# Group 0 in two halves, W on ScalarE's DMA queue, sums three tiles behind, gathers spread over the group two ahead, and a rearranged tail, in a DLRM tower on one core

## The reference

```python
def _cin_layer(X0, Xi, W, b):            # X0 (512,39,16), Xi (512,Fi,16), W (128, 39*Fi)
    Wr = W.reshape(H, F0_, Fi)
    return jnp.einsum('hjk,bjd,bkd->bhd', Wr, X0, Xi) + b[None, :, None]
e = jnp.stack([tbl_0[ids[:, 0]], ..., tbl_38[ids[:, 38]]], axis=1)
# three layers, each summed over d and concatenated: z (512, 384)
h = jnp.concatenate([z, dense_ctx], axis=1)          # (512, 400)
h = jnp.maximum(h @ W_top1 + b_top1, 0.0)            # 512 wide
h = jnp.maximum(h @ W_top2 + b_top2, 0.0)            # 256 wide
y = h @ W_top3
```

## Time and profile before

| | us |
|---|---|
| median of three timed runs | 673.68 (673.07 to 673.69) |
| the profiled execution | 672.67 |
| its span in the profile | 670.6 |
| busy: TensorE / VectorE / ScalarE / GpSimd | 641.9 / 521.2 / 488.3 / 361.1 |
| the first product of group 0's second layer | at 44.37 |
| the last chunk of the last group | at 611.8 |

### The profile page before, as it was taken

How to read it: one execution, slowest core, us unless ns; L and a number is a source line. 1 busy time by engine, 2 the same in 40 slices (tenths; PEclk the granted TensorE clock), 3 DMA queues, 4 the chain that set the end, 5 groups by cost and what they waited for, 6 DMA issues and landing times.

```text
span 670.6 us, 11899 instructions
## 1 busy us (share of the span) xinstructions
PE 641.9 (96%) x2516; PEld 461.4 (69%) x2516; DVE 521.2 (78%) x1478; ACT 488.3 (73%) x1692; POOL 361.1 (54%) x308
## 2 busy tenths in 40 slices
PE   0689999999999999999999999999999999999998
PEld 0246777777777777777777777777777777785483
DVE  0346888878888888888888878888888888897590
ACT  1137877778787868787877878787868787897293
POOL 6878766575656565755666675656575221121000
PEclk9799999999999999999999999999999999999999
DMA  6457687767676777667667767676777657567100
GB/s 225 60 92 168 112 183 133 173 131 162 124 160 128 159 150 163 142 134 155 139 144 134 167 130 161 124 160 129 160 150 162 142 102 178 126 122 215 31 1 0
DMA packets 61944, 91.05 MB, mean 136 GB/s; under 512 B 34599, under 2 KB 38548, under 8 KB 61671
## 3 DMA queue, kind: packets, MB, share of 16 engines
q0 software_dynamic: 14192, 51.02, 42.0%
q1 hardware_dynamic: 47734, 39.85, 21.2%
HBM read 10.59 MB, written 1.28 MB: 18 GB/s over the span
## 4 chain that ended last, share of the span: by engine, by line
PE 91%; POOL 3%; DMA 3%; issue 2%; SPq 1%; ACT 0%; DVE 0%; ACTq 0%; POOLq 0%
PE t_bank L426 22%; PE t_bank L427 21%; PE t_bank L428 21%; PE x_bank L394 14%; PE small_bank L411 5%; POOL emb L324 3%; PE t_bank L491 1%; PE t_bank L471 1%; PE t_bank L502 1%; PE t_bank L503 1%; PE t_bank L514 1%; PE t_bank L505 1%; DMA emb<-in_table,idx 1%; PE x0t_bank L402 1%; DMA emb_scratch<-emb 1%
## 5 line engine op out<-in xcount | busy, mean ns | idle before, releaser
L567 ACT ACTIVATE prod<-t_bank,x0t 128x128 f32<-128x128 f32 x1472 | 417.5, 377 | 114.6 <-PE t_bank L428 109.3
L671 DVE SCALAR_TENSOR_TENSOR prod<-t_bank,x0t,prod 128x128 f32<-128x128 f32 x1024 | 287.9, 343 | 80.1 <-PE t_bank L428 75.8
L426 PE MATMUL t_bank<-w_hi,x_hi 128*128 128x512 f32 (+1 forms) x640 | 307.5, 480 | 0.6 <-DVE x_lo L660 0.3
L427 PE MATMUL t_bank<-w_lo,x_hi 128*128 128x512 f32 (+1 forms) x640 | 247.8, 387 | 0.0
L428 PE MATMUL t_bank<-w_hi,x_lo 128*128 128x512 f32 (+1 forms) x640 | 247.0, 386 | 0.0
L324 POOL DMA_INDIRECT emb<-in_table,idx x160 | 211.8, 1324 | 48.5 <-issue 46.8
L334 POOL TENSOR_TENSOR diag<-x0t,mask 128x320 f32<-128x320 f32 x64 | 87.8, 1372 | 195.4 <-DVE prod L671 97.7
L426 PEld LDWEIGHTS t_bank<-w_hi,x_hi 128*128 128x128 f32 x640 | 120.2, 188 | 54.7 <-issue 29.7
L427 PEld LDWEIGHTS t_bank<-w_lo,x_hi 128*128 128x128 f32 x640 | 120.5, 188 | 47.1 <-issue 25.3
L428 PEld LDWEIGHTS t_bank<-w_hi,x_lo 128*128 128x128 f32 x640 | 120.1, 188 | 24.2
L703 DVE TENSOR_TENSOR prod<-prod 128x768 f32<-128x768 f32 (+2 forms) x192 | 117.4, 611 | 6.0 <-DMA prod<-prod 5.7
(11 more groups left out here) (73 smaller groups left out, 242.8 us busy)
## 6 DMA issues: line engine op xcount, KB each, us to landing
prod<-prod POOLq DMA_DIRECT2D x63, 768.0 KB, 7.1
shared<-rep SPq DMA_DIRECT2D x96, 234.0 KB
shared<-rep SPq DMA_DIRECT2D x48, 78.0 KB
emb<-in_table,idx POOLq DMA_INDIRECT x160
G<-in_w SPq DMA_DIRECT2D x1, 2496.0 KB
rep<-rep SPq DMA_DIRECT2D x28, 78.0 KB
rep<-emb_scratch SPq DMA_DIRECT2D x20, 78.0 KB
prod<-in_w SPq DMA_DIRECT2D x1, 1536.0 KB, 7.1
```

What stands on the lines that cost most here:

```text
L426: pe.matmul(acc, hi, w1_hi[:, cols], start=True, stop=False)
L427: pe.matmul(acc, hi, w1_lo[:, cols], start=False, stop=False)
L567: last = act.activation(prod[:, s, SLOT[c] + u, :], t_bank[c % T_BANKS][:, u * H:(u + 1) * H], ACT.Copy, scale=x0t[:, s, j:j + 1])
L671: last = dve.scalar_tensor_tensor(unit, t_bank[c % T_BANKS][:, u * H:(u + 1) * H], x0t[:, s, j:j + 1], unit, ALU.mult, ALU.add)
```

## The change

Six things are changed.

1. **Group 0 in two parts** of 16 samples (256 columns). Each part has its own ids, 5 gathers, store, load and factors, and own semaphores. The second part's pairs and products are made inside group 0 (p = 7 to 16), and group 1's from p = 21 on.
2. **W** (three loads) is issued from ScalarE's DMA queue and not from SyncE's, and split into hi and lo in four pieces.
3. **BEHIND is 3** and not 2, and `g_product` follows chunk 0 (G_AT) and not chunk 2.
4. **Gathers**: all ten of group g+2 are issued in group g, three each in tiles 0 and 1 and two each in tiles 2 and 3. No gather of group g+3 is issued in group g.
5. **Last tile**: VectorE sums two tiles in it, folds the last tile itself at once, and leaves the tile before for the end.
6. **Tail**: the four products with the 16 dense features use four strips of 32 rows of the array, and one product with G moves behind the long loop, ahead of the wait for z2.

```diff
-BEHIND = 2
+BEHIND = 3
+GATHERS_OF_TILE = [(0, 3), (3, 6), (6, 8), (8, GATHERS)]
-G_AT = 2
+G_AT = 0
 ... (SyncE)
-            x0_of(0, 0, at_once=True)
-            factors(0, 0)
+            store_part(0)
+            load_part(0)
+            store_part(1)
+            factors_of_part(0)
+            load_part(1)
+            factors_of_part(1)
             x0_of(1, 1, at_once=True)
 ... (GpSimd)
-            for g in range(AHEAD):
-                index(g, g)
-                for i in range(GATHERS):
-                    gather(i, g)
+            for part in range(PARTS):
+                gather_part(part)
+            index(1, 1)
+            for i in range(GATHERS):
+                gather(i, 1)
             pool.wait_ge(small_loaded, 16 * SMALL_LOADS)
-            index(AHEAD, 0)
-            for i in range(GATHERS_EARLY):
-                gather(i, 0)
             def group(...):
                 for s in range(TILES_PER_GROUP):
-                    if early and s == INDEX_TILE:
-                        index(g + AHEAD + 1, 1 - half)
+                    if gathers and s == 0:
+                        index(g + AHEAD, half)
                     if fold_before:
                         scaled(t - 1)
                     diagonal(t, s, first)
                     if fold_before:
                         fold((s - 1) % TILES_PER_GROUP)
-                    if gathers and s < INDEX_TILE:
-                        for i in range(GATHERS_EARLY, GATHERS):
-                            gather(i, half)
-                    if early and s >= INDEX_TILE:
-                        for i in range(3 * (s - INDEX_TILE), 3 * (s - INDEX_TILE) + 3):
-                            gather(i, 1 - half)
+                    if gathers:
+                        for i in range(*GATHERS_OF_TILE[s]):
+                            gather(i, half)
 ... (VectorE, the last tile and behind it)
+                            if last and s == TILES_PER_GROUP - 1:
+                                slot = i // 2
+                                for half_of_it in range(2):
+                                    sum_over_j(t - BEHIND + slot, g, slot, 2 * (i % 2) + half_of_it)
-            for i in range(RED):
-                sum_over_j(TILES - 2, GROUPS - 1, 2, i)
             fold_last(TILES - 1, 3)
             for i in range(RED):
-                sum_over_j(TILES - 1, GROUPS - 1, 3, i, by_dve=True)
+                sum_over_j(TILES - 2, GROUPS - 1, 3, i, by_dve=True)
+            for i in range(RED):
+                sum_over_j(TILES - 1, GROUPS - 1, 2, i)
```

More of the change, by code:

```diff
@@ L391, in pair_product @@
                 pe.wait_ge(pair_ready, g * BLOCKS + (b + 1))
-                if b == 0 and not (isinstance(g, int) and g == 0):
+                if b == 0:
                     pe.wait_ge(x1_ready, g)
@@ L395, in pair_product, with part_pair_product, last_part_pair_product, transpose_x0 @@
                           start=b == 0, stop=b == BLOCKS - 1).then_inc(pair_mm, 1)
-            def transpose_x0(half, first):
-                if first:
-                    pe.wait_ge(x0_loaded, 16 * X0_LOADS)
-                for s in range(TILES_PER_GROUP):
+            def part_pair_product(b):
+                pe.wait_ge(early_pair_ready, b + 1)
+                pe.matmul(part_x1, w_pair[:, b * H:(b + 1) * H], pairs[:, b % 2, part_cols(0)],
+                          start=b == 0, stop=b == BLOCKS - 1).then_inc(early_pair_mm, 1)
+            def last_part_pair_product(b):
+                pe.wait_ge(pair_ready, b + 1)
+                pe.matmul(x1_bank[:, part_cols(1)], w_pair[:, b * H:(b + 1) * H], pairs[:, b % 2, part_cols(1)],
+                          start=b == 0, stop=b == BLOCKS - 1).then_inc(pair_mm, 1)
+            def transpose_x0(half, tiles=range(TILES_PER_GROUP), done=x0t_mm):
+                for s in tiles:
                     mm = pe.transpose(x0t_psum[:, s, :], rep[0:F, half, s * P:(s + 1) * P], ident[:, :])
-                mm.then_inc(x0t_mm, 1)
+                mm.then_inc(done, 1)
             def g_product(t, slot):
@@ L594, in _ @@
             act.wait_ge(small_loaded, 16 * SMALL_LOADS)
-            for s in range(TILES_PER_GROUP):
-                copy_x0t(0, s, True)
-            bias_x1(0, True)
-            split_x1_hi(0, 0, True)
+            act.wait_ge(early_x0_loaded, 16 * X0_LOADS)
+            for b in range(2, BLOCKS, 2):
+                act.dma_start(part_second_at(0, b), rep[b:b + PAIRS, 0, part_cols(0)]).then_inc(part_second[b - 1], 16)
+            for s in range(PART_TILES):
+                copy_x0t(0, s, first=True)
@@ L642, in _, with form_part_pairs, split_part_x1_lo, split_last_part_x1_lo @@
         def _(dve):
-            def form_pairs(g, half, b, at_start):
+            def form_part_pairs(part, b):
+                cols = part_cols(part)
+                if b == 0:
+                    dve.wait_ge((early_first_ready, first_ready)[part], 16 * COPIES)
+                else:
+                    dve.wait_ge(part_second[b - 1], 16 * (part + 1))
+                if b >= 2:
+                    dve.wait_ge((early_pair_mm, pair_mm)[part], b - 1)
+                dve.tensor_tensor(pairs[:, b % 2, cols], shared[0:PAIRS, SECOND_SLOTS, cols],
+                                  rep[0:PAIRS, 0, cols] if b == 0 else part_second_at(part, b),
+                                  ALU.mult).then_inc((early_pair_ready, pair_ready)[part], 1)
+            def split_part_x1_lo():
+                cols = part_cols(0)
+                dve.wait_ge(early_x1_hi_ready, 1)
+                dve.tensor_tensor(x1_lo[:, cols], x1[:, cols], x1_hi[:, cols],
+                                  ALU.subtract).then_inc(early_x1_lo_ready, 1)
+            def split_last_part_x1_lo():
+                for i, (a, b) in enumerate(FIRST_PIECES):
+                    dve.wait_ge(x1_hi_ready, i + 1)
+                    dve.tensor_tensor(x1_lo[:, a * P:b * P], x1[:, a * P:b * P], x1_hi[:, a * P:b * P],
+                                      ALU.subtract).then_inc(x1_lo_ready, 1)
+            def form_pairs(g, half, b):
                 if b == 0:
```

305 lines of the change are left out of this document (227 added, 78 removed).

## The result

The changed kernel takes **821.19 us** (median of 4 runs, 819.65 to 823.07), against 673.68 us before (4 runs, 673.07 to 677.39). The ratio is 1.218, with a 95% interval of 1.214 to 1.222: slower by 147.5 us. The forecast was 798 us, in a range of 745 to 850. The profiled execution is that of 819.65 us, with a span of 817.8 us, 147.2 us more than the 670.6 of the earlier trace rows.

What follows compares the result with a forecast made beforehand. TensorE, which never waits in sixteen groups of about 36 us, was taken as the bound, with side jobs covered. 672.67 - 4 (start) - 2 (tail) + 131.6 (group waits) gave 798 us, range 745 to 850.

Steps and rivals of the forecast that it cites:

- The gathers: Groups 1 to 14: late last gather makes TensorE wait, 8.9 us plus 0.5 for the clock, 14 times: 131.6 us.
- the chain from store to first factors: SyncE's store, load, copies and first factors behind the last gather: 16.4 us in the rows.
- Covered: Rival: the late gather stays covered, only start and tail count, 667 us; 5 in 100.
- partly covered: Rival: chain quick, or only part of the 6.2 us ahead of chunk 8 counts, 695 to 737 us; 9 in 100.
- The delay feeds on itself: Rival: load meets tile 3's fold, clock stays at half; above 12.8 us a group, over 850 us; 8 in 100.
- The page's rule: Store to first factors by 2.0 us fixed plus bytes at 436 GB/s: 9.3 us, group loss 1.8, total near 691.
- The clock: Chunks 8 to 10 after the `rep` wait: half clock from about 342 to after 349, costing 0.5 us a group.
- 3 us and more each: Sign: 14 long TensorE waits on `rep` and 14 on VectorE's last sum ahead of the G product, this long.
- The start: Up to the second layer: it starts 7 to 10 us earlier, some given back; net -4 us, bounds -9 and +1.
- what group 0 gives back: Inside group 0: late first pairs of group 1 and queued factors of part 1 return 5 us of the start's gain.
- Three tiles behind: Loop: takes away VectorE's short waits for folds, which TensorE does not see; nothing in itself.
- The tail: Kernel end: long products about 1.1 us sooner, moved product saves 0.8, strips hidden; -2 us, bounds 0 and -4.

Runs made afterwards that it cites:

- run 2: The kernel before with the new gathers alone (ten of group g+2 spread over the four tiles): 801.25 us, ratio 1.189.
- run 1: The changed kernel with the gathers in their old place (nine of group g+3 in tiles 1 to 3, the tenth in tile 0): 677.6 us, ratio 1.005.
- Run 3: The changed kernel with gathers 4, 3, 3, 0 in the four tiles, so the last is in tile 2, not tile 3: 703.0 us, ratio 1.044.
- run 4: The changed kernel with all ten gathers in tiles 0 and 1, five each: 692.26 us, ratio 1.028.
- run 10: The kernel before with BEHIND = 3, the G product behind chunk 0 and the new tail: 673.74 us, ratio 0.999.
- Run 7: The kernel before with W's three loads on ScalarE's queue alone: 680.18 us, ratio 1.008.
- run 6: The changed kernel with W's three loads on SyncE's queue, behind all loads of ids: 814.18 us, ratio 1.207.
- run 9: The changed kernel with early gathers, W on SyncE's queue behind the ids, and the G product behind chunk 2: 677.95 us, ratio 1.005.
- run 5: The changed kernel with the G product behind chunk 2 (p = 12) rather than chunk 0 (p = 10): 840.95 us, ratio 1.246.
- run 11: The kernel before with sums three tiles behind and the rearranged tail, the G product behind chunk 2 as it was: 674.2 us, ratio 1.0005.
- run 12: The kernel before with only the row strips for the dense products and the moved product, still two tiles behind: 672.49 us, ratio 0.998.

## Why the prediction was right, and where it was off

**The gathers: right in place, kind and number.** The prediction had 14 waits for `rep` ahead of chunk 8 and a late VectorE behind them, 9.4 us a group and 131.6 in all. The gathers cost 127.7 us alone (run 2) and 143.6 with the rest of the change around them (run 1). Run 3 shows the cover that the prediction's argument rests on: with 8 us more of it 118 us come back. The prediction put the chain from store to first factors in use at 16.4 us. Measured: 565.10 - 548.29 = 16.8, of which the load took 6.7 where the earlier trace rows gave 5.6, and the copies' start to the factors 3.6. The wait for `rep` is 7.1 (forecast 6.2), the G product 9.5 late (8.9), the loss 9.9 us a group (9.4). So for the fourteen groups this term was 7.5 us too small, 139.1 against 131.6, by the load above all, and it lacked the 5.3 us in group 0; the store was half a microsecond quicker and the last gather's landing, 548.29 - 544.34 = 3.9 us from issue, was near the estimate of 3.6.

**The rivals.** *Covered* and *partly covered* fell with the first profile: the waits are there, 14 of them. *The delay feeds on itself* has its mechanism in part, since the load took 1.1 us more than before, yet a group loses 9.9 us and not the 12.8 from which that rival began. (667 + 14 x 12.8 is 846 and not over 850, a slip without weight here.)

**The page's rule.** By "DMA: Bandwidth & Descriptors" (Anatomy of one DMA) of the Trainium skill, as the prediction worked it out, a group would have lost 1.8 us, and it lost 9.9. The page gives this fit for DMAs that GpSimd issues, and the prediction used it for loads of SyncE's queue. By it a load of 78 KB takes an estimated 2.2 us. The load took 6.7 us, 0.4 us behind a fold, and 5.6 us, 2.6 us behind one, in the earlier trace rows. With the last fold 7.2 us ahead of it, the same load took 2.5 us in the kernel before:

```profile
537.52 0.34 SPq L255 DMA_DIRECT2D rep<-emb_scratch  x1
540.05 3.22 SPq L259 DMA_DIRECT2D rep<-rep  x3
```

So what made the rule fail here is the other traffic, and not the size of the pieces. The prediction went by a row in which the load had met a fold as well. That the row fitted is in part luck: with the 2.5 to 3.0 us of a load that meets none, a group would have lost an estimated 4 us less.

**The clock.** Forecast was half clock from 342 until after 349 in the group shown, 4.4 us into the wait until 5 us beyond it, at a cost of 0.5 us. In the group shown after the change it fell 3 us into the wait and lasted some 6 us beyond it. The chunks 8 to 10 took 4.9 us and not 4, which filled the second wait almost wholly, so the sign "3 us and more each" did not come. The cost is as forecast: a G product 9.5 us late and a loss of 9.9 leave 0.4. In run 2, where the G product does not wait, the half clock is the second part of the loss itself. The prediction compared the wait with the 3.9 us of idle time before the fall at the start; runs 4 and 10 show falls in waits of 2.8 and 3.05 us. This agrees with the clock gate as "TensorE: Matmul & The Clock Gate" of the Trainium skill has it (HAM clock gate): idle brings the half rate back.

**The start: wrong.** "Net -4 us, bounds -9 and +1" measured +10.3 (above). Of these, 5.3 belong to the gathers, so the start itself was out by 9: +5.0, outside its bounds. The second layer starts 2.5 us earlier and not 7 to 10. Two parts of that step failed:

- "W on ScalarE's queue [...] isn't what the start waits for, so nothing is added." Run 7 shows 6.4 us for it in the kernel before, and run 6 gives back 7.0 by the medians in the changed one (2.9 us by the start of the second layer). What I hadn't seen is that W's transfers, issued at the same time on another queue, hold up the ids.
- The 5 us for what group 0 gives back were too few: it is 12.8 (2.5 won and 10.3 lost), and 7.5 without the wait of 5.3. With the ids in time and the gathers early (run 9) the split wins 3.9 us by group 0's chunk 8 and gives back 8.4.

With the terms as measured the sum is 672.67 + 5.0 + 5.3 - 2.2 + 139.1 = 819.9 for the profiled execution, which took 819.65. Of the 21 us between forecast and that time, the start has 9, the gathers' wait in group 0 has 5.3, and the fourteen groups have 7.5.

**Three tiles behind: "nothing in itself" holds only while nothing is late.** With G_AT = 0 TensorE comes to the G product, and so to VectorE's late sum, one place earlier (0.8 us a group with late gathers, run 2 against the changed kernel), and it couples GpSimd's diagonal to the G product of its own tile (run 5). With early gathers its price, if it has one, is within the scatter (runs 10 and 11). That the first of these is the whole of the 0.8 is argued from the rows and wasn't tried alone.

**The tail: right.** From the last group's last chunk to the end there were 670.6 - 611.8 = 58.8 us, and now there are 817.8 - 761.2 = 56.6: -2.2 against -2. The long products start sooner, measured from there, by 1.7 us: 623.04 - 611.8 was 11.2, and 9.6 is the distance now:

```profile
761.17 0.34 PE L536 MATMUL t_bank<-w_hi,x_hi 128*128 128x384 f32 x1
...
770.75 1.55 PE L617 MATMUL t_bank<-G,prod 128*128 128x512 f32 x3 [0.53 <-ACT G L702]
```

## What to carry to other kernels

In a loop whose main engine never waits, find for each side job the chain from its last issue to its first use, and count its cover; the first microsecond beyond it costs its number of groups (here 14), and one tile earlier is worth more (118 us) than all other parts of the change together. A job may be spread within a loop only up to that point. A small transfer on the chain can take twice as long when a big one goes out just ahead of it, so ask of each piece of the chain what stands in front of it. Small loads on which a start hangs go out ahead of big ones on every queue, and a buffer with as many slots as tiles binds the engines together when its reader moves one tile back and stands late in its tile (run 5).

## What the runs showed of the hardware

- Ids of a few KB, issued on SyncE's queue from 0.75 to 2.2 us, landed at 12.8 in the changed kernel, where W's loads went out on ScalarE's queue from 0.7 to 2.2 us; at 3.5 when W was issued behind them (run 6). With two loads of ids issued at 0.76 and 1.18 us beside W they were in at 6.3 (run 7).
- The load of 78 KB in the loop, from its issue to that of the copies which wait for it, took 2.5 to 3.0 us when the last fold (768 KB) had gone out 7 us or more before it, and 2.7 to 3.0 when the fold had gone out at most 0.23 us before. It took 5.0 to 7.2 us when the fold was 0.27 to 3 us ahead. These are 187 of the 190 loads behind 75 us in the traces of all fourteen kernels; the other three lie between (3.9 to 5.4 us ahead: 3.8 to 2.6 us).
- The second gather behind a fold on GpSimd's queue landed 3.9 us after its issue, against 2.76 at the quiet start.
- A gather issued under VectorE's `w_lo` of 4992 columns took 5.3 to 6.4 us; with `w_lo` in pieces of 1280 columns none that began while the pieces ran took over 1.3 in the changed kernel, where I had estimated 2 to 5 us lost; in run 6 two of them took 2.2 and 2.3.
- Four products of 16 rows each in four strips of 32 rows start within 0.02 us and take 1.1 to 1.3 us together (changed kernel, run 12), where one behind the other they took 4.2.
- A wait of TensorE of 2.8 to 3.1 us in a loop at full clock was followed by 3 to 7 us at half clock, and the group lost 1.9 to 3.2 us on top of the wait (three cases, runs 4 and 10).
